# Self attentions: keys spread over 8 heads for two row halves of TensorE, by GpSimd alone, in an unrolled loop

## What is computed

```
Q, K, V = heads(x @ W_Q), heads(x @ W_K), heads(x @ W_V)        # 16 heads of 8
scores = einsum('bhqd,bhkd->bhqk', Q, K) / 8 ** 0.5              # a0: + causal mask
probs  = softmax(scores)
out    = einsum('bhqk,bhkd->bqhd', probs, V)
```

## Time and profile before

| what | us |
|---|---|
| median of 3 runs | 1338.86 (1338.19 to 1339.38) |
| profiled execution, its own time | 1333.34 |
| span of the profiled execution | 1331.1 |
| a0, from the end of V's projections to the last normalise | 59.9 |
| a1, the same | 49.0 |
| a2, from the sum columns to the last normalise | 68.1 |

### The profile page before, as it was taken

One profiled execution on the slowest core, in us unless ns is written; L12 is line 12 of the kernel. 1 busy time (PEld: TensorE's weight loads), 2 busy tenths in 40 slices (PEclk: granted clock), 3 DMA queues, 4 the chain that ended last, 5 costly groups with the idle time before them and its releaser, 6 DMA issues.

```text
span 1331.1 us, 22303 instructions
## 1 busy us (share of the span) xinstructions
PE 1041.1 (78%) x9246; PEld 741.0 (56%) x9246; DVE 715.7 (54%) x1194; ACT 496.4 (37%) x649; POOL 225.6 (17%) x202
## 2 busy tenths in 40 slices
PE   3776765898873599999999999997575546739888
PEld 2455444787761266666666666665344333438767
DVE  3234775433343566666766666670585478763221
ACT  0235231222222156656656666655032202403333
POOL 2000460121213001111111111110161003400110
PEclk9898786999995689999999999999697767759999
DMA  8683000110201423323432332220001000000110
GB/s 270 202 347 131 1 0 1 31 41 24 97 0 50 151 104 129 106 103 114 148 122 104 122 113 104 103 76 18 1 1 32 1 0 0 1 0 16 33 47 16
DMA packets 41347, 98.48 MB, mean 74 GB/s; under 512 B 9976, under 2 KB 24960, under 8 KB 41264
## 3 DMA queue, kind: packets, MB, share of 16 engines
q1 hardware_dynamic: 41264, 97.29, 21.4%
HBM read 55.49 MB, written 0.73 MB: 42 GB/s over the span
## 4 chain that ended last, share of the span: by engine, by line
PE 50%; issue 16%; DVE 14%; ACT 7%; POOL 6%; SPq 3%; DMA 2%; POOLq 0%; DVEq 0%
PE PS L262 49%; DVE kl L1500 3%; ACT kh L1090 2%; ACT PT L1103 2%; DVE prT L1504 2%; POOL work_area L390 2%; SPq L905 2%; DVE mx L1515 2%; POOL PT L390 1%; DMA ctxT<-in_ctx_T 1%; DVE x L675 1%; POOL blank_g L257 1%; POOL rstd_all L281 1%; PE PS L292 1%; ACT work_area L654 1%
## 5 line engine op out<-in xcount | busy, mean ns | idle before, releaser
L1515 DVE TENSOR_REDUCE mx<-PS 128x2 f32<-128x1024 f32 x192 | 230.7, 1216 | 85.0 <-PE PS L262 84.9
L1103 ACT ACTIVATE PT<-PS 128x1024 f32<-128x1024 f32 (+1 forms) x208 | 212.3, 1021 | 94.7 <-PE PS L262 93.5
L262 PE MATMUL PS<-QB,QS 128*128 128x512 f32 x576 | 159.1, 425 | 23.9 <-DVE wcol L663 21.9
L262 PE MATMUL PS<-QB,KS 128*128 128x256 f32 (+1 forms) x832 | 166.2, 322 | 10.0 <-ACT PT L1103 9.5
L262 PEld LDWEIGHTS PS<-QB,QS 128*128 128x128 f32 x576 | 109.8, 201 | 61.0 <-issue 27.0
L262 PEld LDWEIGHTS PS<-QB,KS 128*128 128x128 f32 (+1 forms) x832 | 115.9, 186 | 43.8 <-issue 31.6
L262 PE MATMUL PS<-PT,work_area 128*32 128x128 f32 (+1 forms) x3328 | 134.4, 279 | 0.5 <-ACT PT L1103 0.5
L262 PE MATMUL PS<-KS,QB 64*128 64x512 f32 (+1 forms) x512 | 109.8, 458 | 13.1 <-DMA KS<-kl 9.5
L675 DVE SCALAR_TENSOR_TENSOR x<-PS,wcol,x 128x128 f32<-128x128 f32 x128 | 44.9, 351 | 138.2 <-PE PS L262 134.8
L262 PEld LDWEIGHTS PS<-PT,work_area 128*32 128x32 f32 (+1 forms) x3328 | 78.4, 109 | 46.3 <-issue 42.9
L262 PE MATMUL PS<-nat_area,work_area 128*128 128x128 f32 (+2 forms) x928 | 85.0, 275 | 13.7 <-DVE work_area L670 5.9
(11 more groups left out here) (241 smaller groups left out, 1408.8 us busy)
## 6 DMA issues: line engine op xcount, KB each, us to landing
KS<-kh SPq DMA_DIRECT2D x32, 800.5 KB
ctxT<-in_ctx_T SPq DMA_DIRECT2D x24, 800.5 KB, 4.5
nat_area<-in_ctx_tiles SPq DMA_DIRECT2D x16, 832.0 KB, 6.8
KS<-kl SPq DMA_DIRECT2D x16, 800.5 KB
work_area<-in_ctx_T SPq DMA_DIRECT2D x8, 800.5 KB, 10.2
nat_area<-in_L_ffn_experts_w SPq DMA_DIRECT2D x24, 256.0 KB, 3.2
nat_area<-in_L_ffn_W SPq DMA_DIRECT2D x16, 256.0 KB, 3.0
KS<-mask_parts SPq DMA_DIRECT2D x32, 50.1 KB
```

The source lines that it names most:

```text
L262: return T.matmul(o, l, r, start=start, stop=stop, **k)
L1103: P["exp_a"].done(S.activation(PT[0:rows, par, :], PS[0:rows, 1024:2048], ACT.Exp), f"e{k}")
L1515: ins = V.reduce_max(by_pair[:, :, j // 3, j % 3:j % 3 + 1], src, AX)
```

## The change

The keys of 8 heads, not 16, are spread in each buffer, but for both halves of the partitions: partitions 0 to 63 hold heads 0 to 7, partitions 64 to 127 heads 8 to 15, and a new constant mask (`C_HM8`) has 8 columns. A buffer for a whole tile has 1024 columns. GpSimd alone fills it, with one instruction a tile, in four buffers in turn. TensorE computes the scores in four matmuls of 64 rows and 64 columns of its array; the two row halves write different PSUM banks. Queries are read from `Q_all` directly. The values of the stage are written with a stride of 18, so that the sum columns stand between them for all tiles at once, and ScalarE copies no values. All tiles are unrolled. TensorE's order becomes weighted values of t−1, transposes of t, scores of t+2; VectorE's becomes `subtract_max` of t, `normalise` of t−2. ScalarE's is copy of t−1, exponential of t.

```diff
-        V_all = early[:, 512:512 + 2 * TOKENS]
+        V_all = early[:, 512:512 + 2 * PAIRS * 144].rearrange("p (g b c) -> p g b c", g=2 * PAIRS, b=8)
...
+        SPREAD = [a[:, 1024 * t:1024 * t + 1024] for a in (tail_area, PT[:, :, :].rearrange("p a n -> p (a n)")) for t in range(2)]
...
+            def scores(t):
+                L = LANE[t % 2]
+                at(T, st + "_g", f"kbd{t}")
+                if t >= 2:
+                    at(T, st + "_v", f"sub{t - 2}")
+                for r in range(2):
+                    rows = slice(64 * r, 64 * r + 64)
                     for g in range(2):
-                        last = mm(PS[SEQ * g:SEQ * g + SEQ, 512 * (L["bank"] + c):512 * (L["bank"] + c) + 512],
-                                  L["q"][:, SEQ * g:SEQ * g + SEQ], L["kbd"][:, 1024 * g + 512 * c:1024 * g + 512 * c + 512])
+                        o = 512 * (L["bank"] + r)
+                        last = mm(PS[SEQ * g:SEQ * g + SEQ, o:o + 512],
+                                  Q_all[rows, 128 * t + SEQ * g:128 * t + SEQ * g + SEQ],
+                                  SPREAD[t % 4][rows, 512 * g:512 * g + 512], tile_position=(64 * r, 64 * g))
...
+            scores(0)
+            scores(1)
+            for t in range(PAIRS):
+                if t >= 1:
+                    weighted(t - 1)
+                transposed(t)
+                if t + 2 < PAIRS:
+                    scores(t + 2)
+            weighted(PAIRS - 1)
...
         def attn_scalar(st, scale=1.0):
-                    P[st + f"_a{lane}"].done(
-                        S.activation(LANE[lane]["values"].rearrange("p (b c) -> p b c", c=18)[:, :, 0:16],
-                                     V_all[:, bass.ds(512 * i + 256 * lane, 256)].rearrange("p (b c) -> p b c", c=16),
-                                     ACT.Copy), "values")
...
+            for t in range(PAIRS):
+                if t >= 1:
+                    copied(t - 1)
+                pr = LANE[t % 2]["pr"]
+                at(S, st + "_v", f"sub{t}")
+                P[st + "_a"].done(S.activation(pr, pr, ACT.Exp, scale=scale), f"exp{t}")
+            copied(PAIRS - 1)
...
         def attn_gpsimd(st):
+            for t in range(PAIRS):
+                at(G, st + "_v", "k" if st == "a2" else f"k{t // 4}")
+                if t >= 4:
+                    at(G, st + "_s", f"s{t - 4}")
+                every = [128, 2, 8, SEQ]
+                P[st + "_g"].done(G.tensor_tensor(
+                    SPREAD[t % 4].rearrange("p (g h k) -> p g h k", g=2, h=8),
+                    K_all[:, 128 * t:128 * t + 128].rearrange("p (g k) -> p g k", g=2).unsqueeze(2).broadcast_to(every),
+                    consts[:, C_HM8:C_HM8 + 8].unsqueeze(1).unsqueeze(3).broadcast_to(every), ALU.mult), f"kbd{t}")
...
         def heads_vector(st, mask, unit=None):
-            def keys(i, lane):
-                L = LANE[lane]
-                vdone(V.tensor_copy(L["q"], Q_all[:, bass.ds(256 * i + 128 * lane, 128)]), st + f"_k{lane}", "q", i)
-                P[st + f"_k{lane}"].done(spread_keys(V, L["kbd"], 2 * i + lane, 0), "kbd")
...
+            for t in range(PAIRS):
+                subtract_max(t)
+                if t >= 2:
+                    normalise(t - 2)
+            for t in (PAIRS - 2, PAIRS - 1):
+                normalise(t)
```

More of the change, by code:

```diff
@@ L338, in two_tiles @@
[L338 to L362, removed]
+            T.wait_ge(sum_columns, int(st[1]) + 1)
+            def scores(t):
[5 more added lines that the diff above has]
+                    rows = slice(64 * r, 64 * r + 64)
+                    for g in range(2):
+                        o = 512 * (L["bank"] + r)
+                        last = mm(PS[SEQ * g:SEQ * g + SEQ, o:o + 512],
+                                  Q_all[rows, 128 * t + SEQ * g:128 * t + SEQ * g + SEQ],
+                                  SPREAD[t % 4][rows, 512 * g:512 * g + 512], tile_position=(64 * r, 64 * g))
+                P[st + "_s"].done(last, f"s{t}")
@@ new lines, in transposed, with weighted @@
+            def transposed(t):
+                L = LANE[t % 2]
+                at(T, st + "_a", f"exp{t}")
+                if t >= 2:
+                    at(T, st + "_v", f"o{t - 2}")
+                for b in range(8):
+                    o = 512 * (L["bank"] + 2) + 128 * b
+                    last = T.transpose(PS[:, o:o + 128], L["pr"][:, 128 * b:128 * b + 128], ident)
+                P[st + "_t"].done(last, f"pT{t}")
+            def weighted(t):
+                L = LANE[t % 2]
+                at(T, st + "_a", f"pT{t}")
+                for b in range(8):
+                    for g in range(2):
+                        o = 512 * (L["bank"] + 2) + 18 * b
+                        last = mm(PS[SEQ * g:SEQ * g + SEQ, o:o + 18],
+                                  L["prT"][:, 128 * b + SEQ * g:128 * b + SEQ * g + SEQ], V_all[:, 2 * t + g, b, :])
+                P[st + "_o"].done(last, f"o{t}")
@@ L368, in heads_done @@
             else:
[L369 to L370 removed]
+                at(eng, st + "_v", f"o{PAIRS - 1}")
         def attn_scalar(st, scale=1.0):
[L373 to L376, removed]
[L378 to L384 removed]
@@ L386, in spread_keys, with copied @@
-        def spread_keys(eng, dst, tile, g):
-            hm = head_mask.unsqueeze(2).broadcast_to([128, HEADS, SEQ])
-            src = K_all[:, bass.ds(128 * tile + SEQ * g, SEQ)].unsqueeze(1).broadcast_to([128, HEADS, SEQ])
-            return eng.tensor_tensor(dst[:, 1024 * g:1024 * g + 1024].rearrange("p (h k) -> p h k", h=HEADS), src, hm, ALU.mult)
-        def attn_gpsimd(st):
-            with G.Fori(0, PAIRS // 2) as i:
-                for lane in range(2):
-                    at(G, st + f"_k{lane}", "q", i)
-                    apart_g(i, lane)
-                    P[st + f"_g{lane}"].done(spread_keys(G, LANE[lane]["kbd"], 2 * i + lane, 1), "kbd")
+            def copied(t):
+                at(S, st + "_t", f"pT{t}")
+                if t >= 2:
+                    at(S, st + "_o", f"o{t - 2}")
+                b = 512 * (LANE[t % 2]["bank"] + 2)
+                P[st + "_a"].done(S.activation(LANE[t % 2]["prT"], PS[:, b:b + 1024], ACT.Copy), f"pT{t}")
@@ L468, in two_tiles @@
-            def two_tiles(i):
-                for lane in range(2):
-                    subtract_max(i, lane)
-                    if not (isinstance(i, int) and i == ROUNDS - 1):
-                        keys(i + 1, lane)
-                    if lane == 1:
-                        normalise(i, 0)
-                    elif not (isinstance(i, int) and i == 0):
-                        normalise(i - 1, 1)
-            for lane in range(2):
-                keys(0, lane)
+                                    s2.unsqueeze(3).broadcast_to([128, 8, 2, HD]), ALU.mult), f"o{t}")
@@ L1653, in constants @@
     c[:, C_ONE] = 1.0
+    c[:, C_HM8:C_HM8 + 8] = (p[:, None] % 64) // HD == np.arange(8)[None]
     c[:, C_HEAD:C_HEAD + 2] = p[:, None] // 64 == np.arange(2)[None]
```

88 lines of the change are left out of this document (35 added, 53 removed).

## The result

The changed kernel takes 1296.86 us (median of 4 runs, 1293.70 to 1300.14); the kernel before, run beside it, 1338.53 (4 runs, 1334.08 to 1339.38). The ratio is 0.9695, 95% interval 0.9657 to 0.9734: faster by 41.7 us between the medians. Between the two profiled executions the span fell from 1331.1 to 1292.4 us, by 38.7. Forecast was 28.

A forecast was written before the change was run, and what follows sets the result against it. A tile costs VectorE's work, the busiest engine in the three self attentions, plus its waits. Gains of 18.1 us in the tile steps and 10.0 at the starts make 28: 1338.9 − 28 = 1311 us, range 1294 to 1330.

The forecast's parts named there:

- rival A: All three self attentions: the clock stays full, tiles of 4.8, 3.4 and 5.2 us, gain 39 to 44; chance 0.17.
- the starts: Start of each attention: earlier masking or fewer VectorE operations, shorter first scores; 3.4, 3.4 and 3.2 us, together 10.0.
- seven steps: First to eighth tile of each attention: tiles of 5.3, 4.0 and 5.6 us, a gain of 18.1 us.
- the sum columns behind GpSimd: Start of a2: the copy of the sum columns may wait behind GpSimd's first keys, 1.9 us.
- The third switch of tile shape: TensorE between scores and weighted values: a drain of 0.1 to 0.2 us a tile, 2.4 to 5 us on 24 tiles.
- Rival C: Scores: row halves do not overlap, keeping 1.94 and 3.68 us; gain falls by some 9, 1320 us; chance 0.07.
- my signs: What the trace would show if right: attention spans of about 51, 41 and 56 us, scores at 1.1 us.
- Port waits: VectorE's subtractions in a0 and a2 wait for GpSimd's shared access: 0.4 us a tile, bounds 0 and 1 us.
- The clock share: TensorE's share of time at the full clock: 0.5 in a0, 0.75 in a1, 0.5 in a2.
- 4.8, 3.4, 5.2 us: Tile times at the full clock in a0, a1, a2: VectorE sets the first and third, TensorE the second.
- At the low clock TensorE sets all: 5.8, 5.8, 6.0: Tile times in us at the low clock in a0, a1, a2, with TensorE's work setting each.
- B: All three attentions: the clock stays low, tiles of 5.8, 5.8 and 6.0 us, gain 9, 1330 us; chance 0.15.

The follow-up runs named there:

- rows_apart: The changed kernel, but TensorE waits for the first row half's scores to end before starting the second's; 1362.11 us, 1.0195 of the kernel before.

## Why the prediction was right, and where its size was off

**The number.** The gain of 16 to 36 us that I called the forecast (1303 to 1323) was missed: it is 41.7 us between the medians, 38.7 between the profiles. The measured 1296.86 us lies in the stated range of 1294 to 1330 only because the range reached down to rival A, and A, a clock that stays full, did not happen. That part is luck. What was forecast and came is the mechanism: VectorE relieved of the keys, scores in 1.09 us, GpSimd off the path behind the starts but for its port stalls, and masking at the end of V's matmuls.

**The sum.** It had 18.1 us for seven steps and 10.0 for the starts; measured are 9.1 + 7.8 + 14.2 = 31.0 and 4.0 + 3.4 + 2.0 = 9.4, with the last tiles 0.6 longer: 39.9 us.

**The starts** were right in a0 and a1, within 0.6 us. In a2 I expected 3.2 us and got 2.0. The bound that I named, the sum columns behind GpSimd, was not it (that copy took 0.29 us); GpSimd came out of its all-reduce late. The same 7.09 us stood ahead of its first work in a2 in the kernel before, and I had not looked.

**GpSimd, scores, switches.** 1.88 to 1.90 us for a tile's keys where nothing is in the way, 1.09 and about 1.98 for the scores, 0.09 for a switch: all as taken. The third switch of tile shape, for which I had 0.1 to 0.2 us a tile, is at most 0.09 us in that row. Rival C is excluded by the changed trace. I had also priced it wrongly: with its own tiles it costs 7 x (0.85 + 0.95 + 0.75) = 17.9 us and not 9, so it would have stood near 1330 us; and the stage of a0 in my signs should have been 52 us, not 51.

**Port waits** of 0.4 us a tile in a0: eight subtractions sum to 12.7 us where eight of 1.23 make 9.8, so 0.36 a tile. In a2 I had 0.55 (5.2 − 4.65), and it was (11.9 − 9.8 + 0.7)/8 = 0.35. VectorE's own tile was 4.14 us (169.97 to 174.11) in a0 and 4.41 (1111.84 to 1116.25) in a2 instead of 4.4 and 4.65: its instructions follow without the gaps that I added.

**The clock share** I had chosen as 0.5, 0.75, 0.5, from the clocks of whole stages. Over the seven steps alone, the windows of the changed kernel are:

```profile
141.57:174.11 32.54, 23.34 (x296) 14.09 (x288) 30.38 (x32) 12.75 (x13) 18.85 (x13) 0.84 0.01 1
956.34:981.21 24.87, 21.61 (x264) 13.11 (x256) 19.32 (x24) 11.95 (x13) 7.79 (x5) 0.86 0.01 2
1082.29:1116.25 33.96, 27.97 (x296) 16.52 (x288) 31.51 (x36) 13.56 (x13) 17.23 (x10) 0.72 0.01 1
```

The kernel before had 0.88, 0.98 and 0.78 over its own seven steps, more than the 0.82, 0.90 and 0.71 of its stages, which I had used. (clock − 0.5)/0.5 gives 0.68, 0.72, 0.44 after the change. With my tiles these shares make 7 x (0.83 + 0.59 + 1.22) = 18.5 us, hardly more than 18.1. So the choice of clock is not what was mis-sized.

**The mis-sized terms.** The seven steps were to take 7 x (5.3 + 4.0 + 5.6) = 104.3 us and took 32.5 + 24.9 + 34.0 = 91.4. VectorE's waits for scores that stand at or behind a low stretch are these (in brackets; the second row is a mask add that did not wait):

```profile
151.74 1.23 DVE L448 TENSOR_TENSOR work_area<-PS,consts 128x1024 f32<-128x1024 f32 x1 [1.51 <-PE PS L261]
...
165.40 1.22 DVE L448 TENSOR_TENSOR work_area<-PS,consts 128x1024 f32<-128x1024 f32 x1
...
963.00 1.22 DVE L450 TENSOR_REDUCE smax<-PS 128x16 f32<-128x1024 f32 x1 [1.79 <-PE PS L261]
...
968.38 1.22 DVE L450 TENSOR_REDUCE smax<-PS 128x16 f32<-128x1024 f32 x1 [2.42 <-PE PS L261]
...
1091.89 1.23 DVE L448 TENSOR_TENSOR work_area<-PS,consts 128x1024 f32<-128x1024 f32 x1 [0.49 <-PE PS L261]
...
1097.53 1.22 DVE L448 TENSOR_TENSOR work_area<-PS,consts 128x1024 f32<-128x1024 f32 x1 [1.14 <-PE PS L261]
```

Most of the 12.9 us were in the tiles at the full clock, "4.8, 3.4, 5.2 us". VectorE's own work in a0 is five tiles of 4.14 and the first two, which have no normalisation behind them, of 3.70: 28.1 us, where I had 7 x 4.4 = 30.8. In a2 it is 29.5 us instead of 32.6. In a1 the steps without the two long waits sum to 20.7 us instead of 7 x 3.4 = 23.8: the first takes 2.40, the last three TensorE's 3.25. Port waits took 1.1 us less in a2. That is some 9.8 us in all.

The low clock makes up the other 3.2. "At the low clock TensorE sets all: 5.8, 5.8, 6.0" was charged with 3.5, 4.2 and 2.8 us; the waits above are 1.5, 4.2 and 1.6. It was right in a1 and too dear in a0 and a2. Where the low clock lasts over two tiles, the step does come near TensorE's (5.38 us from 963.00 to 968.38, 5.64 from 1091.89 to 1097.53, and 7.67 throughout in rows_apart). Where it lasts for less, VectorE does not see it: the scores at 163.23, at the low clock, end at 165.22, and VectorE takes them up at 165.40. In a0 and a2 TensorE has that slack, since its 3.25 us at the full clock are less than VectorE's tile; in a1 it has none. The slack as the reason is argued from these rows; no run took it away.

**What was left out.** I gave the order inside a tile no price, since I costed the new tile from its parts and not as a difference. The runs make a square of sums: 180.0 us before unrolled, 187.6 with the new order alone, 160.1 with the new spreading alone, 144.4 with both. So of the 39.9 us about 4 are the unrolling (put at nothing, wrongly), 20 the spreading in the old order, and 16 the order on top of it. The order gives that only together with the new spreading; that VectorE's keys between a subtraction and a normalisation are what stood against it is argued from the 19.1 us of waits. The values' copy was nothing, as said.

**The rivals.** Had the low clock held (B), the tile would have been TensorE's 5.8 us. It did not, though scores stream half as long. What keeps the low clock away is not shown; the rows show only that 2.4 GHz came back where the four quarter matmuls ran at once, and in the kernel before with two matmuls of 128 rows, and hardly ever in rows_apart, with two quarter matmuls at a time (0.50 to 0.52).

## To carry to other kernels

Count an engine's own tile from its rows instruction by instruction, and give the first tiles a term of their own: that was more of the error here than the clock was. A bound from an engine's work at its slow clock holds only where the slow stretch outlasts the engine's slack. Moving work off the busiest engine can pay more when the waits that it covered are reordered too (16 us of 39.9 here), so price the order of the queue along with the work, and expect the parts not to add. Look at what the receiving engine did just before: here it stood still for 7 us after an all-reduce, in the trace of the kernel before already.

## What was not expected of the hardware

TensorE busy without a gap for 48 us (149.50 to 197.47 in a0 of rows_apart) stayed at 1.2 GHz, while with the scores issued twice, four matmuls at a time, the clock was 0.88, 0.94, 0.79 instead of 0.85, 0.84, 0.68. The Trainium skill ("TensorE: Matmul & The Clock Gate", Loop structure matters more than you think) makes warmth a matter of whether matmuls stay back to back; the matmuls of rows_apart do, and their row does not agree. In a2 GpSimd's first ordinary operation starts 6.8 to 7.1 us after the end of the all-reduce in all fourteen traces of this case, with VectorE's masking before it or beside it. And eight VectorE scalings of 128x128 from SBUF to SBUF took 9.40 us instead of 2.14 beside GpSimd's splits, a loss of 7.3 us, where the same splits cost the tiles of a0 1.3 us.
